# Two sets of mask multiplications of a chunked scan move from GpSimd to VectorE

## What is computed

```python
x = x + 0.5 * _L0_ffn_ref(_layernorm(x, axis=-1), L0_ffn_rhs)
x = x + _L0_attn_ref(_layernorm(x, axis=-1), ...)
x = x + 0.5 * _L0_ffn_ref(_layernorm(x, axis=-1), L0_ffn_rhs)
```

```python
def step(h, inp):
    qt, kt, vt, gt = inp
    h = h * jnp.exp(gt)[..., None] + kt[..., None] * vt[..., None, :]
    ot = jnp.einsum('bhk,bhkv->bhv', qt * scale, h)
    return (h, ot)
```

## Time and profile before

| | us |
|---|---|
| median of 2 runs | 3341.74 |
| the two runs | 3346.28, 3337.20 |
| the profiled execution | 3365.09 |
| its span on the slowest core (core 4) | 3363.4 |
| spans of the other seven cores | 3320.0 to 3358.5 |

### The profile page before, as it was taken

The page is one execution under the profiler, slowest core; times in us unless marked ns, Lnnn a source line. Parts: engine busy times, 40 slices in busy tenths (PEclk is TensorE's granted clock), DMA queues, the critical chain, the costliest instruction groups (busy, mean ns, idle before and its releaser), DMA issues.

```text
span 3363.4 us, 25064 instructions; the slowest of 8 cores (3320.0 to 3363.4 us)
## 1 busy us (share of the span) xinstructions
PE 1597.5 (47%) x7145; PEld 878.0 (26%) x7218; DVE 1059.9 (32%) x2471; ACT 515.5 (15%) x1117; POOL 478.4 (14%) x979
## 2 busy tenths in 40 slices
PE   2002526354644554455454554555465536554664
PEld 1001313132322322232323232323142313222331
DVE  2514141323054205321531144114412440343043
ACT  0011111112021202120211021111111121112021
POOL 0004450000130012011201120112012101110130
PEclk9997757576867686767676767677777767776777
DMA  2343522020310131124012301230123003100310
GB/s 76 117 133 110 168 92 91 3 75 26 100 50 19 45 113 37 45 62 128 4 38 75 101 1 38 76 100 1 38 76 100 13 25 111 64 13 25 125 51 13
DMA packets 104456, 216.73 MB, mean 64 GB/s; under 512 B 16480, under 2 KB 41072, under 8 KB 104320
## 3 DMA queue, kind: packets, MB, share of 16 engines
q1 hardware_dynamic: 71072, 107.10, 10.3%
q0 software_dynamic: 28928, 92.30, 8.6%
q10 hardware_dynamic: 4320, 15.73, 1.4%
HBM read 189.89 MB, written 25.17 MB: 64 GB/s over the span
## 4 chain that ended last, share of the span: by engine, by line
PE 43%; DVE 18%; DMA 8%; ACT 7%; issue 7%; DVEq 4%; SPq 2%; POOL 2%; ACTq 1%; POOLq 0%
PE PF L493 13%; PE PF L761 5%; PE PP L472 4%; DVEq L141 4%; PE PF L395 4%; PE PA L472 3%; DMA WH<-wgh 2%; DVE YSC L730 2%; PE PA L637 2%; DMA WH<-wvh 2%; PE PO L395 2%; DMA WL<-wvl 2%; SPq L453 2%; PE PP L514 2%; PE PO L663 2%
## 5 line engine op out<-in xcount | busy, mean ns | idle before, releaser
L493 PE MATMUL PF<-WH,U2TH 128*128 128x512 bf16 x570 | 168.2, 436 | 301.9 <-DMA WH<-wgh 105.4
L385 PE MATMUL PT<-IDFB,T1SC 128*128 128x128 bf16 x176 | 25.7, 300 | 510.7 <-DVE T1SC L372 492.7
L338 DVE TENSOR_TENSOR ST<-ST 128x1 f32<-128x1 f32 x38 | 6.0, 159 | 748.7 <-ACT ST L301 748.7
L493 PEld LDWEIGHTS PF<-WH,U2TH 128*128 128x128 bf16 x608 | 62.7, 107 | 391.3 <-issue 341.9
L622 POOL TENSOR_TENSOR QX<-QTE,QMASK 128x128 f32<-128x128 f32 x256 | 103.9, 440 | 421.8 <-DVE QTE L616 421.8
L597 PE MATMUL PT<-IDF,KHT 128*128 128x128 f32 x32 | 13.1, 410 | 306.3 <-DVE KHT L594 306.3
L427 PE MATMUL PT<-IDF,YSC 128*128 128x128 f32 x176 | 47.8, 427 | 229.7 <-ACT YSC L421 160.3
L493 PE MATMUL PF<-WL,U2TH 128*128 128x512 bf16 x608 | 153.9, 399 | 0.4 <-DMA WL<-wgl 0.4
L457 POOL DMA_DIRECT2D WL<-wkl x64 | 33.8, 536 | 843.8 <-PE PA L472 843.6
L385 PEld LDWEIGHTS PT<-IDFB,T1SC 128*128 128x128 bf16 x176 | 15.3, 126 | 527.7 <-issue 527.7
L493 PE MATMUL PF<-WH,U2TL 128*128 128x512 bf16 x608 | 143.6, 379 | 0.0
(11 more groups left out here) (213 smaller groups left out, 3448.6 us busy)
## 6 DMA issues: line engine op xcount, KB each, us to landing
WH<-wvh SPq DMA_DIRECT2D x88, 256.0 KB, 7.0
WL<-wvl POOLq DMA_DIRECT2D x64, 256.0 KB, 9.0
WL<-wgl POOLq DMA_DIRECT2D x64, 256.0 KB, 6.9
WH<-wgh SPq DMA_DIRECT2D x64, 256.0 KB, 9.4
WL<-wol POOLq DMA_DIRECT2D x64, 256.0 KB, 7.7
WH<-woh SPq DMA_DIRECT2D x64, 256.0 KB, 9.6
XR<-x ACTq DMA_DIRECT2D x22, 512.0 KB, 8.2
WH<-wkh SPq DMA_DIRECT2D x88, 128.0 KB, 3.5
```

The lines of the kernel that those rows point to most:

```text
L493: la=(ci == 2 and dt == 7): e.matmul(PF[:, nb * 512:(nb + 1) * 512], xop[:, dt * R + i * 128: dt * R + (i + 1) * 128], wop[:, dt * D + nb ...
```

## The change

The steps of L622 (QX) and L647 (HSX) are given to VectorE in place of GpSimd. They stay where they are in the order of the steps; operands, shapes and masks are the same.

```diff
                 def _qx(mc, st_):
                     for hh in range(4):
-                        b.step("gpsimd", lambda e, mc=mc, hh=hh: e.tensor_tensor(
+                        b.step("vector", lambda e, mc=mc, hh=hh: e.tensor_tensor(
                             QX[mc % 2][:, hh * 128:(hh + 1) * 128], QTE[mc % 2][:, :],
                             QMASK4[:, hh * 128:(hh + 1) * 128], ALU.mult),
...
                 def _hsx(mc, st_):
                     for hh in range(4):
-                        b.step("gpsimd", lambda e, mc=mc, hh=hh: e.tensor_tensor(
+                        b.step("vector", lambda e, mc=mc, hh=hh: e.tensor_tensor(
                             HSX[mc % 2][:, hh * DV:(hh + 1) * DV],
                             HS[:, mc * DV:(mc + 1) * DV],
                             HMASK[:, hh * DV:(hh + 1) * DV], ALU.mult),
```

## The result

The changed kernel takes 3478.1 us (median of 11 runs, 3463.9 to 3539.7) against 3352.2 us for the kernel before (10 runs, among them the two shown above). The ratio is 1.0396, 95% interval 1.0348 to 1.0444: **slower by 4.0%, some 132 us**. The medians are of all executions; the ratio leaves out those in which one die ran long at a lower granted clock. The forecast was 94 us more, a time of 3436 us, in a range up to 3476. The direction and the waits came true; the term for TensorE's clock was half of what it measured.

A forecast was written before the change was run, and what follows sets the result against it. The prediction took a chain of hand-overs between engines to bound the kernel. Waits of 62 us plus 32 us for TensorE's clock made 94 us on the 3341.7 us median, 3436 us, with a range of 3392 to 3476.

The forecast's parts named there:

- What bounds the kernel: Scan pairs: one thread of hand-overs between engines, none near full; what each of 32 pairs loses, the span loses.
- Part one, QX: Eight QX on VectorE between QTE and KHT, 0.20 us apart, start TensorE's first product 0.28 us later by pair.
- neither bound: VectorE's moved instructions: 0.33 us apart would add 1.8 us by pair (59 us); halved column time would save 0.7 (22 us).
- Part two, HSX: Eight HSX on VectorE behind the second AM start the output block 1.65 us later, 1.37 behind that AM.
- One sign: Expected in the profile after: L655 waits for HSX, 1.65 us behind the second product's end, in all 32 pairs.
- The waits together: Added waits at the first product and the output block: 1.93 us by pair, 62 us in 32 pairs.
- Part three, the clock: Output blocks on TensorE: the clock sometimes rises late or falls in the gap, mean 1.0 us by pair, 32 us.
- the waits alone: Rival: output blocks keep their clock and only 62 us are left, 3404 us, 1.9% more; chance 0.17.
- The bound for a whole block at half the clock: Clock term's upper bound: a whole output block at half the clock loses 3.7 us by pair.
- The clock is lost throughout: Rival: every output block at 1.2 GHz for two thirds or all of its work, 141 to 179 us; chance 0.10.
- The clock is won: Rival: full clock lasts into the next pair's products, leaving about 6 us, 3348 us; chance 0.04.
- The faster engine wins: Rival: GpSimd's speed bounds the pair, so QX on VectorE gives 51 us, 3291 us, 1.5% less; chance 0.02.

The follow-up runs named there:

- filler kernel: Changed kernel with L605's state product repeated on TensorE ahead of the output block, while it waits for HSX; ratio 1.0208 to the kernel before.
- carried-clock kernel: Interleaved order plus a repeat of the KHT and QX products behind each chunk's first output block; 3309.1 us, ratio 0.9840 to the kernel before.
- interleaved order: Changed kernel with HSX ahead of the first AM and each group's second KHT directly behind its four QX; 3316.4 us, ratio 0.9903 to the kernel before.

## Why the prediction was right and wrong, point by point

**What bounds the kernel** was right: a thread of hand-overs. A loss in a pair was a loss in the span (126 us by pairs, 132 by the ratio).

**Part one, QX**, forecast 0.28 us later, measured 0.32. QX went 0.20 apart: eight took 1.70 us with a mean of 0.284. The nearest row, AM's price per column, was the right one to follow; neither bound (0.33 apart, half the column time) came near.

**Part two, HSX**, forecast 1.65 us later and 1.37 behind the second AM, measured 1.68 and 1.37 to 1.40 in most pairs (1.40 on average). One sign was put wrongly: L655 stands 1.5 us behind the second product's end and not 1.65, since before it had started 0.2 us ahead of that end (994.66 against 992.95 + 1.91). The mean of one HSX is 216 ns against the 0.22 taken. The waits together, forecast 62 us, are 64.

**Part three, the clock**, is the step that failed: the mean loss by pair, taken as 1.0 us from the one block of the last round with 0.78. It is 2.03 us, 1.76 in the block and 0.27 in the products ahead of it, and 1.93 us of it reach the end of the pair: 62 us, not 32. The choice went wrong in two ways. The row came from a kernel without a gap, where the clock always rises late in the products or early in the block; the changed kernel puts idle time both ahead of the products and ahead of the block, and the experiments show that the two act on each other (22 and 81 us alone, 126 together). And the products ahead got no term of their own, though a part of the second product had been at the high level (895 ns before, 1046 after). The rivals framed the truth: "the waits alone" (62 us) is nearly what the filler kernel measured (67), and the block's mean of 5.58 lies in the middle between 3.75 and 7.17 us. The bound for a whole block at half the clock, 3.7 us, stood in the text (it measures 3.42), and the range did not go far enough towards it.

The Trainium skill describes such a loss in "TensorE: Matmul & The Clock Gate", section "HAM oscillation — how this bites in real kernels": waits between bursts of products bring the low clock back in each iteration, and each iteration pays for it. The runs agree in part: a block takes 1.76 us more on average, but 27% of the blocks are as short as at full clock.

Of the 42 us between the forecast of 3436 and the median of 3478, some 10 are none of the three parts: the kernel before itself has a median of 3352 in ten runs, against 3342 in the two that were shown.

**The other rivals.** "The clock is lost throughout" was too much: 27% of the blocks kept it. "The clock is won" did not occur here (a granted clock of 0.51 in the products after, 0.56 before), but the carried-clock kernel shows that it can be had in part. "The faster engine wins" fell in this kernel for the reason given, KHT behind all eight QX and HSX behind AM; in the interleaved order VectorE's speed does win, 0.49 us by pair at the first product (2.33 to 1.84) and 1.0% in all. So the rule on engine selection was not wrong on this work. The place in the list was what the change had got wrong. One chance was booked wrongly: this rival's own 51 us, 1.5%, lie within 2%, so its 0.02 belonged there and not under faster.

GpSimd's absence was put at nothing for the time. The KHT that had run beside GpSimd's QX did go from 398 to 281 ns, and the forecast of the first product, which has no term for it beyond a KHT of 0.29 us, came out within 0.04 us. The Trainium skill's "GPSIMD Engine Reference", section "1. Specifications", says that GpSimd shares its SBUF interfaces with VectorE and contends with instructions of two SBUF inputs. The two means agree with that; no run here separates it from other effects of GpSimd's work.

## What to carry to other kernels

Moving work to a faster engine is a question of where it stands in that engine's list: put each step where the engine waits anyway, and directly ahead of what needs it. The same instructions on VectorE gave 4.0% more time with HSX behind AM, and 1.0% less with HSX ahead of AM and QX interleaved with KHT. Where TensorE works in short bursts, price an added wait in two terms: its length, and the clock of the burst behind it. Here the two were of the same size, 64 and 62 us.

## What the runs showed that I had not expected

Products that nobody reads are worth time on TensorE. Taking L605 out of the kernel before cost 0.65%, and 64 repeats of it in the gap of the changed kernel took its loss from 4.0 to 2.1%. Waits on the way to a burst do not add: +22 us and +81 us alone, +126 together. And the same wait of 1.48 us had different outcomes in one kernel: the clock was kept, fell within the block, rose during the wait itself, or stayed low through most of the block. So one pair read in order of time can't give the price of a wait on TensorE; in this case it took the mean over all pairs and cores.
